# The causal mask of the straight scores: a ScalarE copy into PSUM in place of TensorE mask products

## What is computed

```python
qkv = hidden_states @ w_attn + b_attn          # 4 batches x 256 tokens, 32 heads of 16
scores = einsum('bqhd,bkhd->bhqk', q, k) * SCALE
rel = pos[None, :] - pos[:, None]
causal = rel <= 0
scores = where(causal, scores + slopes * rel, -inf)
attn = softmax(scores, axis=-1)
out = einsum('bhqk,bkhd->bqhd', attn, v)
x = x + out @ w_proj + b_proj
```

## Time and profile before

| | |
|---|---|
| median of 3 runs | 714.89 us (714.68 to 716.71) |
| profiled execution, its own time | 714.72 us |
| its span | 713.0 us, 10154 instructions |
| mean granted clock of TensorE | 0.983 of full speed |
| busy share of the span | PE 92%, PEld 68%, DVE 67%, ACT 48%, POOL 12% |

### The profile page before, as it was taken

One profiled execution on the slowest core, in us unless ns is written; L12 is line 12 of the kernel. 1 busy time (PEld: TensorE's weight loads), 2 busy tenths in 40 slices (PEclk: granted clock), 3 DMA queues, 4 the chain that ended last, 5 costly groups with the idle time before them and its releaser, 6 DMA issues.

```text
span 713.0 us, 10154 instructions
## 1 busy us (share of the span) xinstructions
PE 658.1 (92%) x3784; PEld 486.1 (68%) x3784; DVE 476.4 (67%) x905; ACT 343.3 (48%) x536; POOL 84.7 (12%) x185
## 2 busy tenths in 40 slices
PE   5895999999998889999989999999999999999997
PEld 4783678678676567887776665756757555787875
DVE  6555495696589769787694655274463797868555
ACT  5221734613634663442357996485582924435221
POOL 4411002102100020100133000100100120100000
PEclk9987999999999999999999999999999999999999
DMA  8494423321744240000143000000001304000000
GB/s 269 123 276 123 116 63 89 94 90 56 236 124 151 106 151 9 0 1 1 25 169 126 0 1 0 1 0 1 0 1 42 136 0 177 2 29 16 16 30 30
DMA packets 31763, 51.35 MB, mean 72 GB/s; under 512 B 3433, under 2 KB 17132, under 8 KB 30159
## 3 DMA queue, kind: packets, MB, share of 16 engines
q1 hardware_dynamic: 31330, 49.12, 21.4%
q10 hardware_dynamic: 384, 1.57, 1.0%
HBM read 42.09 MB, written 8.40 MB: 71 GB/s over the span
## 4 chain that ended last, share of the span: by engine, by line
PE 76%; DVE 13%; ACT 4%; DMA 2%; issue 2%; POOL 1%; SPq 1%; ACTq 1%; DVEq 0%; POOLq 0%
PE ps L1815 12%; PE ps L1848 11%; PE ps L2040 11%; PE ps L1979 10%; PE ps L1678 6%; PE ps L1983 5%; PE ps L1756 2%; DVE nmax L1072 2%; PE ps L1746 2%; PE ps L1660 2%; PE ps L1824 2%; PE ps L1694 2%; DVE prodT L1587 1%; ACT sign_junk L966 1%; DVE x_sb L1416 1%
## 5 line engine op out<-in xcount | busy, mean ns | idle before, releaser
L2040 PE MATMUL ps<-wdT,prodT 128*128 128x512 f32 (+1 forms) x176 | 77.7, 597 | 0.4
L795 ACT ACTIVATE probsT<-ps 128x1536 f32<-128x1536 f32 x32 | 46.2, 1450 | 38.2 <-PE ps L1746 38.0
L2040 PEld LDWEIGHTS ps<-wdT,prodT 128*128 128x128 f32 (+1 forms) x176 | 32.8, 190 | 40.7 <-issue 38.3
L834 ACT ACTIVATE funs<-ps 128x512 f32<-128x512 f32 x16 | 9.6, 598 | 91.8 <-PE ps L1817 80.9
L667 POOL TENSOR_SCALAR ln_spread<-ln_moments 128x1 f32<-128x1 f32 x24 | 8.5, 354 | 298.4 <-DVE ln_moments L1143 298.3
L1149 DVE SCALAR_TENSOR_TENSOR junk<-x_sb,gate_row 128x512 f32<-128x512 f32 x48 | 41.2, 859 | 1.0
L1587 DVE COPY prodT<-ps 128x512 f32<-128x512 f32 (+1 forms) x24 | 13.7, 599 | 40.4 <-PE ps L2029 40.0
L1072 DVE TENSOR_REDUCE nmax<-ps 128x4 f32<-128x1024 f32 x32 | 38.8, 1213 | 0.0
L1416 DVE SCALAR_TENSOR_TENSOR x_sb<-b_row,coef,x_sb 128x512 f32<-128x512 f32 x48 | 36.2, 754 | 1.8
L901 ACT CAST aT_hi<-ps 128x512 fp32r<-128x512 f32 x32 | 17.2, 590 | 38.1 <-PE ps L1824 38.1
L966 ACT ACTIVATE sign_junk<-mlp_size_next,minus_guess 128x1376 bf16<-128x1376 f32 x24 | 34.6, 1443 | 0.8
(11 more groups left out here) (280 smaller groups left out, 1720.5 us busy)
## 6 DMA issues: line engine op xcount, KB each, us to landing
cuts<-parts SPq DMA_DIRECT2D x16, 384.0 KB, 3.2
qst<-cuts SPq DMA_DIRECT2D x48, 128.0 KB, 2.7
w_first_raw<-in_L_ffn_w SPq DMA_DIRECT2D x6, 1024.0 KB, 8.0
w_second_raw<-in_L_ffn_w SPq DMA_DIRECT2D x6, 1024.0 KB, 8.6
kst<-cuts SPq DMA_DIRECT2D x36, 128.0 KB, 2.6
wqkv_raw<-in_L_attn_a_w_attn SPq DMA_DIRECT2D x3, 1024.0 KB, 8.2
wdT<-in_L_attn_b_w_down SPq DMA_DIRECT2D x1, 2560.0 KB, 10.0
wg_raw<-in_L_attn_b_w_gate SPq DMA_DIRECT2D x1, 2048.0 KB, 8.1
```

The lines of the kernel that those rows point to most:

```text
L795: nc.scalar.activation(probsT[:, g % 2, :].rearrange("p (k n) -> p k n", k=3), slot[g % 2], ACT.Exp).then_inc(exp_ok.sem, 1)
L2040: last = nc.tensor.matmul(ps[:, Y_BANK, :], prodT[0:m, c, :], wdT[0:m, c, :], start=(c == 0), stop=(c == IC - 1))
```

## The change

From the second batch on (b >= 1), the mask of the straight scores is no longer written by TensorE. A tile `seed` of 128 x 1536 in bf16, as wide as a slot, is filled once by GpSimd: zeros by a memset, and the mask by four copies, placed between the two mask constants. ScalarE copies it into the slot (`seed_scores`) when the slot's last reader is done, and TensorE's eight products add to it after a wait for `seeded`. The copies stand at fixed places of ScalarE's queue: seed 0 of the next batch ahead of the exponential of group 7, seed 1 behind it, seeds 2 and 3 ahead of the two parts of `turned_heads`, 4 ahead of `turned_rows`, 5 and 6 behind it, 7 behind the next batch's `second_part` 0. In batch 3, seeds 5 to 7 stand one ahead of each `weight_high`. `gate_means` moves from ahead of `first_part(b + 1, 0)` to behind seed 7, ahead of `first_part(b + 1, 1)`. Batch 0 keeps its mask products.

```diff
+        seed = sb("seed", [P, 3, 2, 2, P], BF16)
...
+        seeded = sig("seeded", NG)
+        seed_set = sem("seed_set")
...
                 nc.gpsimd.affine_select(out=maskS[:, :], in_=maskS[:, :], compare_op=ALU.is_ge, fill=NEG,
                                         base=0, pattern=[[-1, P]], channel_multiplier=1).then_inc(consts, 1)
+                nc.gpsimd.memset(seed[:, 1:3, :, 0, :], 0.0).then_inc(seed_set, 1)
+                pool.wait_ge(consts, 8)
+                for k in range(2):
+                    nc.gpsimd.tensor_copy(seed[:, 0, :, k, :], maskS[:, :].unsqueeze(1).broadcast_to([P, 2, P])
+                                          ).then_inc(seed_set, 1)
+                    nc.gpsimd.tensor_copy(seed[:, 1 + k, :, 1, :], maskS[:, :].unsqueeze(1).broadcast_to([P, 2, P])
+                                          ).then_inc(seed_set, 1)
...
+            def seed_scores(b, g):
+
+                if g >= 2:
+                    need(act, max_ok, b, 2 * (g - 1))
+                else:
+                    need(act, exp_ok, b - 1, NG - 1 + g)
+                nc.scalar.copy(slot[g % 2], seed[:, :, :, :, :].rearrange("p s h k n -> p s (h k n)")
+                               ).then_inc(seeded.sem, 1)
+
+            def turned_heads(b, js=range(TB)):
+                for j in js:
...
             def attend(b):
                 for g in range(NG):
+                    if g == NG - 1 and b < B - 1:
+                        seed_scores(b + 1, 0)
                     need(act, sT_ps, b, g + 1)
...
+                if b < B - 1:
+                    seed_scores(b + 1, 1)
...
+            act.wait_ge(seed_set, 5)
             for b in range(B - 1):
...
                 if b >= 1:
-                    turned_heads(b - 1)
+                    for j in range(TB):
+                        seed_scores(b, 2 + j)
+                        turned_heads(b - 1, (j,))
+                    seed_scores(b, 4)
                     turned_rows(b + 1)
+                    seed_scores(b, 5)
+                    seed_scores(b, 6)
+                first_part(b + 1, 0)
+                second_part(b + 1, 0)
+                if b >= 1:
+                    seed_scores(b, 7)
                 if b == 1:
                     gate_means()
-                first_part(b + 1, 0)
-                second_part(b + 1, 0)
                 first_part(b + 1, 1)
                 second_part(b + 1, 1)
...
-            turned_heads(B - 2)
+            for j in range(TB):
+                seed_scores(B - 1, 2 + j)
+                turned_heads(B - 2, (j,))
+            seed_scores(B - 1, 4)
             need(act, v_out, B - 1, TB)
             for e in range(E):
+                seed_scores(B - 1, 5 + e)
                 weight_high(w1_first, w1_here, w1_high, 0, e)
...
                 sl = slot[g % 2]
-                if g >= 2:
-                    need(pe, max_ok, b, 2 * (g - 1))
-                nc.tensor.matmul(sl[:, 0, :].rearrange("p (h k) -> p h k", h=G), ident16[:, :], diagonal(maskS, G),
-                                 start=True, stop=False, skip_group_check=True)
-                for s in range(2):
-                    nc.tensor.matmul(sl[:, 1 + s, :].rearrange("p (h k) -> p h k", h=2)[:, :, P:S], ident16[:, :],
-                                     diagonal(maskS, 2), start=True, stop=False, skip_group_check=True)
+                if b >= 1:
+                    need(pe, seeded, b - 1, g + 1)
+                else:
...
```

More of the change, by code:

```diff
@@ L743, in turned_rows @@
                                    row_banks(b)[j].rearrange("p (c t) -> p c t", c=KC)).then_inc(hT_ok.sem, 1)
-            def turned_heads(b):
-                for j in range(TB):
+            def seed_scores(b, g):
[7 more added lines that the diff above has]
+                for j in js:
                     bank = work[1 - j] if b < B - 1 else work[j]
@@ L1705, in scores @@
                 sl = slot[g % 2]
-                if g >= 2:
-                    need(pe, max_ok, b, 2 * (g - 1))
-                nc.tensor.matmul(sl[:, 0, :].rearrange("p (h k) -> p h k", h=G), ident16[:, :], diagonal(maskS, G),
-                                 start=True, stop=False, skip_group_check=True)
-                for s in range(2):
-                    nc.tensor.matmul(sl[:, 1 + s, :].rearrange("p (h k) -> p h k", h=2)[:, :, P:S], ident16[:, :],
-                                     diagonal(maskS, 2), start=True, stop=False, skip_group_check=True)
+                if b >= 1:
+                    need(pe, seeded, b - 1, g + 1)
+                else:
+                    if g >= 2:
+                        need(pe, max_ok, b, 2 * (g - 1))
+                    nc.tensor.matmul(sl[:, 0, :].rearrange("p (h k) -> p h k", h=G), ident16[:, :], diagonal(maskS, G),
+                                     start=True, stop=False, skip_group_check=True)
+                    for s in range(2):
+                        nc.tensor.matmul(sl[:, 1 + s, :].rearrange("p (h k) -> p h k", h=2)[:, :, P:S], ident16[:, :],
+                                         diagonal(maskS, 2), start=True, stop=False, skip_group_check=True)
                 for i in range(G):
```

## The result

The changed kernel takes **729.94 us** (median of 4 runs, 729.05 to 734.35), the kernel before 715.8 in the runs beside it: a ratio of **1.021, 95% interval 1.018 to 1.024**. The forecast was 728.4. The profiled execution took 729.34 us with a span of 727.5, against 714.72 and 713.0 before, so the traces differ by 14.6 us. The mean granted clock of TensorE is 0.969 instead of 0.983.

The account below looks back on a forecast made before the run. TensorE was taken to bound batches 1 and 2, VectorE batch 3. First stage 1.8, batch 1 6.35, batch 2 0.8 and batch 3 4.75 us sum to 13.7, so 714.7 + 13.7 = 728.4 us, range 720.5 to 733.5.

Parts of the forecast that it names:

- The path: Straight scores: masks removed save at most 10.3 us of TensorE, counting only where the rest waits for TensorE.
- Batch 1: Second attention stretch: +4.4 us from gate_means behind seed 7 and +1.95 from the clock, together +6.35.
- The walk: Batch 1 followed step by step through the engines' queues, with start and end times, from maximum 3 to turned_part(2,3).
- The clock's part: Batch 1, behind TensorE's wait of 4.1 us: work at half rate loses 1.95 us, bounds 0 and 3.4.
- Batch 3: Last attention stretch: seeds alternating with weight casts cost 2.8 us, project_heads at half rate 1.95; +4.75, bounds 1.5 and 6.2.
- Batch 2: Third attention stretch, without gate_means: the wait for seed 5 costs 1.1 us; +0.8 in all, bounds 0 and 2.8.
- rival (c): Batches 1 and 2: the clock falls also on the 2 us waits for seed 5; up to 732.3 us, chance 0.12.
- The first stage: Constants at the start: GpSimd's added memset and copies hold up VectorE's cast; +1.8 us, bounds 0 and 2.8.
- rival (a): First stage: VectorE's cast gets in between GpSimd's instructions and nothing is lost; 726.6 us, chance 0.15.
- the two large terms: The forecast losses of batch 1, +6.35 us, and batch 3, +4.75 us.

Follow-up runs that it names:

- seed_1_to_4: The changed kernel with seeds only for groups 1 to 4 of batches 1 to 3, and gate_means in batch 0: 714.15 us, ratio 0.997.
- gate_early: The changed kernel with gate_means moved to batch 0, ahead of the copy of the maxima; all seeds stay: 725.24 us, ratio 1.011.
- gate_only: The kernel before, with only gate_means moved as in the change, behind second_part(2,0), and no seeds: 719.16 us, ratio 1.005.
- busy_waits: The changed kernel with TensorE products that nobody reads put into its long waits in batches 1 and 3: 726.31 us, ratio 1.015.
- no_seed_b3: The changed kernel with its mask products back in batch 3, seeds only in batches 1 and 2: 725.13 us, ratio 1.013.
- casts_apart: The changed kernel with batch 3's ScalarE order changed to seeds 5, 6, cast 0, seed 7, cast 1: 730.8 us, ratio 1.020.
- text_last: The kernel before, with GpSimd's two-input subtraction for text moved behind its 31 one-element memsets: 717.52 us in one run.
- seed_1_busy: As seed_1, with TensorE products that nobody reads put into batch 0's long waits: 715.46 us, ratio 0.999.
- seed_1: The changed kernel with a seed only for group 1 of batches 1 to 3, and gate_means in batch 0: 715.26 us, ratio 0.999.

## Why the prediction was right, and where it wasn't

**The path, right.** That the masks' 10.3 us would not be won held. seed_1_to_4 shows it in the small: twelve masks removed without harm, 5.2 us of TensorE, bring 0.3% in the total, and 1.8 us by the end of the attention. One reading of the prediction needs a limit: that TensorE is nearly always busy in batches 1 and 2 doesn't make each of its masks count there, since its waits for VectorE grew by as much as a mask each.

**Batch 1, right: 6.35 forecast, 6.0 measured.** The walk held step by step: maximum 3 100.94 (100.8 forecast), seed 5 102.79 (102.7), first_part(2,0) 108.05 (108.05), second_part 109.83 (109.8), end of seed 7 111.8 (111.8), gate_means 111.73 to 117.7 (111.7 to 117.6), residue 118.50 (118.5), TensorE 119.43 (119.5). gate_early and gate_only show that the term belongs to the place of gate_means behind seed 7. The clock's part was put at 1.95 and was 1.6 by the time from the start of turned_part(2,3) to the turn (4.47 instead of 2.84), 1.5 by busy_waits.

**Batch 3, right: 4.75 forecast, 4.4 measured.** Seeds and casts alternate as walked, and no_seed_b3 shows that all of it comes from the seeds. The split was less exact: the last pair of reductions starts in the end 3.4 us later than before plus the shift (230.25 - 8.1 - 218.76), where 2.8 was put, since the scores ahead of it also ran at half rate, and the clock took 1.0 more in project_heads, where 1.95 was put; together 1.6 by busy_waits. Another 0.6 behind the turn I hadn't counted: the DMAs of the maxima took SyncE 2.44 us to issue instead of 1.79, and TensorE waited 1.39 us for them instead of 0.75. It is no part of the change as such, since gate_early and busy_waits have 1.79 there; why it comes and goes is open.

**Batch 2, mis-sized: 0.8 forecast, 2.1 measured,** inside its bounds. The step that failed is the clock after the wait for seed 5, which I had set at full: TensorE waited 1.85 us, began turned_part(3,0) at 166.65, and from 167.5 to 170.9 it ran at half rate, four products in 1.05 us:

```profile
166.65 0.72 PE L1713 MATMUL ps<-rowsT_hi,wqkv_hi 128*128 128x256 f32 x4
...
167.86 1.05 PE L1713 MATMUL ps<-rowsT_lo,wqkv_hi 128*128 128x256 f32 x4
```

That cost 1.5 us; without it the batch would have cost 0.5. This is rival (c). In batch 1 of the changed kernel a wait of 1.89 us at the same place brought no fall, in gate_early it did. The walk also lacked a wait of 1.92 us for seed 2 of this batch (up to 157.49), of which little was left, as the wait for VectorE behind it shrank from 1.06 to 0.18.

**The first stage, wrong: 1.8 forecast, nothing measured.** The step that failed is the reading of one row: that VectorE's cast had waited for GpSimd's whole run of constants. In the changed kernel the cast took 0.17 us while seed copies ran, and it was GpSimd that waited, at its second operation beside VectorE's long one:

```profile
12.57 0.17 DVE L1195 CAST bias_parts<-bias_cols 128x16 bf16<-128x16 f32 x1
...
13.64 2.44 DVE L1072 SCALAR_TENSOR_TENSOR wqkv_lo<-wqkv_raw,wqkv_hi 128x2048 fp32r<-128x2048 f32 x1
```

```profile
12.61 0.39 POOL L644 COPY seed<-maskS 128x256 bf16<-128x256 bf16 x1
...
13.65 0.28 POOL L646 TENSOR_SCALAR_AFFINE_SELECT maskT<-maskT 128x128 bf16<-128x128 bf16 x1
13.90 2.34 POOL L648 TENSOR_SCALAR_AFFINE_SELECT vision<-vision 128x128 f32<-128x128 f32 x1
```

Its constants ended at 18.2 us, ahead of the next thing it had to do (19.68), so nobody was late: rival (a). residue(0,0) even began 0.34 us earlier than before (17.24 against 17.58). The size of the added work was right (a memset 0.52 and four copies of 0.39, 2.1 us). The Trainium skill (SBUF — State Buffer, Who interferes with whom) has the port pair held for one instruction by the engine that issued first; that rule would have given nothing here, and both the cast of 0.17 and the 2.34 us agree with it. The operation of 0.28 us ahead of the latter doesn't quite: by the trace it started 0.01 us behind VectorE's long one and wasn't held. Why the cast of the kernel before took 1.80 us, longer than the 0.45 of the one two-input operation beside it, is open; text_last shows only that it goes when that operation goes.

**Not foreseen: 1.6 us behind the attention.** I had all that follows move along. In the changed kernel the clock was low from 263.0 to 266.4, where before it wasn't. Ahead of it TensorE had only short waits, of 0.93, 1.19 and 0.66 us. No experiment isolates it. It doesn't look like the change's own: busy_waits, casts_apart and the other runs made from the changed kernel, with the same code there, don't have it, and text_last, made from the kernel before, has one at the same products (251.5 to 254.7).

That the sum came out only 0.9 below the profiled time is in part luck, since errors of both signs met: 1.8 too much in the first stage, and 1.3, 0.6 and 1.6 too little in batch 2 and behind the turns of batch 3, against 0.7 too much in the two large terms.

## What to carry to other kernels

An instruction taken off the busiest engine is worth only what that engine's own wait doesn't give back: look at the idle time and releaser ahead of its next instruction. Work handed to a less busy engine is paid by what stands behind it in that queue, so walk the queue, and look for long instructions that nobody waits for and that a new order puts in front of urgent ones. A wait of TensorE costs its own length, and then sometimes again what the next products lose at half rate; a small change's total moves with that, so judge it by the positions in the trace and by many runs.

## What the runs showed of the hardware

- ScalarE copies 128x1536 from bf16 in SBUF to float32 in PSUM in 1.44 us, as long as the exponential of as many float32 elements from PSUM (1.45): no gain from the two-byte input shows.
- Products of TensorE that nobody reads can pay: 37 of them made the changed kernel 3.6 us faster. In seed_1_busy 51 of them won 2.0 us where they stood, and a fall of the clock 45 us later, which seed_1 doesn't have, and a longer wait took it back.
- After waits of about 2 us the clock sometimes fell and sometimes didn't: it stayed up behind 2.17 us in gate_only, and fell behind 1.85 us in batch 2 of the changed kernel. Each fall cost 0.5 to 1.7 us, and they account for some 6 of the 14.6 us by the rows: 1.6 in batch 1, 1.5 in batch 2, 1.6 in batch 3, 1.6 later. Behind the same wait of 3.4 us near 267 to 269 us, the clock was low for some 4 us of the work in the kernel before and for some 6 in seed_1_to_4, which cost 1.1 us more.
- VectorE's casts of 0.17 us pass between GpSimd's copies and memsets. GpSimd's operations of 0.29 and 0.45 us took 2.34 and 2.01 beside a long two-input operation of VectorE.
